# First attention: the head sums, the lead of VectorE's sums and products, and the fetch of rows one by one

## What is computed

```python
h = jnp.maximum(_layernorm(x, axis=-1), 0.0)
x = x + _L0_gnn_ref(h, src, dst, ...)        # gatv2 with 8 heads, layer norm, gatv2 with 1 head, layer norm
h = jnp.maximum(_layernorm(x, axis=-1), 0.0)
x = x + _L1_gnn_ref(h, edge_index, edge_type_34, ...)

def gatv2(x, src, dst, Ws, bs, Wd, bd, attn):
    H, D = attn.shape
    fs = (x @ Ws + bs).reshape(-1, H, D)
    fd = (x @ Wd + bd).reshape(-1, H, D)
    e = jax.nn.leaky_relu(fs[src] + fd[dst], 0.2)
    logits = jnp.einsum('ehd,hd->eh', e, attn)
    m = jax.ops.segment_max(logits, dst, num_segments=N)
    ex = jnp.exp(logits - m[dst])
    denom = jax.ops.segment_sum(ex, dst, num_segments=N)
    alpha = ex / denom[dst]
    out = jax.ops.segment_sum(alpha[:, :, None] * fs[src], dst, num_segments=N)
    return jax.nn.elu(out)
```

## Time and profile before

| | |
|---|---|
| median of 3 runs | 3938.12 us (3933.74 to 3942.07) |
| the profiled execution | 3949.69 us, of it 3948.0 us span |
| busy of the span | TensorE 3111.3 (79%), VectorE 2549.2 (65%), ScalarE 1629.4 (41%), GpSimd 1508.1 (38%) |
| stages, us from the start | first attention 400 to 1090, projections 1090 to 1300, second attention 1300 to 1810, relations 1810 to 3230, last gather 3230 to 3705, the rest to 3948 |

### The profile page before, as it was taken

One profiled execution on the slowest core, in us unless ns is written; L12 is line 12 of the kernel. 1 busy time (PEld: TensorE's weight loads), 2 busy tenths in 40 slices (PEclk: granted clock), 3 DMA queues, 4 the chain that ended last, 5 costly groups with the idle time before them and its releaser, 6 DMA issues. The chain is left out here.

```text
span 3948.0 us, 63256 instructions
## 1 busy us (share of the span) xinstructions
PE 3111.3 (79%) x14356; PEld 2365.0 (60%) x14357; DVE 2549.2 (65%) x5088; ACT 1629.4 (41%) x4996; POOL 1508.1 (38%) x1783
## 2 busy tenths in 40 slices
PE   0196788888869799995669999999999974444699
PEld 0053444444445455553359999999999973444455
DVE  8233799999856788886645555555455548999412
ACT  0010566666622222222324444444444438888400
POOL 0373454545346666662111111111111127777200
PEclk6598899999989899997879999999999986666799
DMA  0233433434354455552145656556555545555300
GB/s 25 78 85 105 130 117 113 123 110 119 97 204 156 154 160 152 157 160 97 48 153 184 184 182 185 171 180 186 177 182 180 180 136 169 176 176 176 132 9 31
DMA packets 181911, 546.64 MB, mean 138 GB/s; under 512 B 37415, under 2 KB 82299, under 8 KB 181563
## 3 DMA queue, kind: packets, MB, share of 16 engines
q0 software_dynamic: 77264, 331.42, 28.1%
q1 hardware_dynamic: 53772, 143.14, 11.9%
q10 hardware_dynamic: 50832, 71.59, 5.0%
HBM read 428.42 MB, written 117.91 MB: 138 GB/s over the span
## 5 line engine op out<-in xcount | busy, mean ns | idle before, releaser
L1795 PE MATMUL pO<-wh,gT 128*128 128x384 f32 x4128 | 1096.8, 339 | 3.7 <-DVE wl L1833 3.7
L1795 PEld LDWEIGHTS pO<-wh,gT 128*128 128x128 f32 x4128 | 752.7, 189 | 4.5 <-DVE wl L1833 4.5
L1795 PE MATMUL pO<-wl,gT 128*128 128x384 f32 x2064 | 692.9, 336 | 0.0
L798 POOL DMA_INDIRECT row<-fs_d,rec x400 | 460.5, 1151 | 385.9 <-PE pA L977 232.1
L1819 DVE TENSOR_SCALAR cntge<-pT 128x768 int32<-128x768 int32 x173 | 165.7, 958 | 574.7 <-PE pT L504 573.8
L511 PE MATMUL pO<-wt,hT 128*128 128x384 f32 (+1 forms) x1200 | 418.9, 511 | 43.0 <-ACT hT L1501 19.6
L1747 ACT ACTIVATE gT<-cntge 128x256 fp32r<-128x256 f32 x1038 | 371.7, 410 | 172.3 <-PE pO L1795 122.8
L923 ACT ACTIVATE sj<-sj 128x96 f32<-128x96 f32 x1176 | 313.2, 268 | 210.3 <-DVE sj L1032 207.4
L1795 PEld LDWEIGHTS pO<-wl,gT 128*128 128x128 f32 x2064 | 390.2, 189 | 0.0
L1757 ACT ACTIVATE nrow<-pO 128x384 f32<-128x384 f32 x344 | 165.9, 482 | 543.1 <-PE pO L1795 543.1
L1927 PE MATMUL pC<-identb,own 128*128 128x128 bf16 x960 | 193.1, 304 | 236.0 <-ACT cntge L1908 121.9
(11 more groups left out here) (335 smaller groups left out, 5686.3 us busy)
## 6 DMA issues: line engine op xcount, KB each, us to landing
raw<-in_L_gnn_W_rel_dram SPq DMA_DIRECT2D x204, 384.0 KB
y_d<-nrow ACTq DMA_DIRECT2D x344, 192.0 KB
y_d<-nothing SPq DMA_DIRECT2D x53, 384.0 KB
row<-fs_d,rec POOLq DMA_INDIRECT x400
kept_d<-fdt ACTq DMA_DIRECT2D x1, 3840.0 KB, 16.3
kept<-kept_d SPq DMA_DIRECT2D x1, 3840.0 KB
fs_d<-of SPq DMA_DIRECT2D x9, 388.0 KB
fd_d<-of SPq DMA_DIRECT2D x9, 388.0 KB, 2.6
```

What stands on the lines that cost most here:

```text
L798: pool.indirect_dma_start(b["row"][u][:, j, :], None, table, bass.IndirectOffsetOnAxis(ap=b["rec"][u][:, 2 * j + field:2 * j + field + 1], ...
L1795: last = pe.matmul(pO[:, q, 0:HALF], gT[:, c, half, :].bitcast(F32R), w[:, c, lo:up].bitcast(F32R), start=c == 0 and k == 0, stop=c == KC ...
```

## The change

Three things in the first attention, and one in the shared gather:

1. ScalarE makes the head sums of all four rows (32 activations a group). VectorE's L1029 goes, and with it the signal `own_ok`. The products come in the order of rows 2, 3, 0, 1, where it was 1, 2, 3, 0.
2. `sj` becomes two buffers. VectorE's `add` and ScalarE's `sums` run for group u+2 in iteration u, not u+1, and once more ahead of the loop. The wait on `logits` is for the group two back.
3. TensorE's program keeps its order: pS of u+2, pA of u.
4. Where `used` counts once a row (first attention and last gather), GpSimd waits for each row's own count before its fetch, not for all four before the first. The second attention keeps its one wait.

The parts that `attention` had for one head go; no call used them.

```diff
-            def rows(u):
+            def rows(u, free=None):
                 for j in range(S):
+                    if free is not None and used.rate == S:
+                        used.wait(pool, *free, j + 1)
+                        pool.sem_inc(b["posted"], 1)
                     pool.indirect_dma_start(b["row"][u][:, j, :], None, table, bass.IndirectOffsetOnAxis(
...
-                    used.wait(pool, i, w - U)
+                    if used.rate == 1:
+                        used.wait(pool, i, w - U)
                     pool.sem_inc(b["posted"], 1)
-                    rows(w % U)
+                    rows(w % U, (i, w - U))
...
-            BY_DVE = 1 if heads > 1 else 0
-
-            ORDER = [*range(BY_DVE, S), *range(BY_DVE)]
+
+            ORDER = [*range(S // 2, S), *range(S // 2)]
...
-                sj = sb("sj", [P, S, D], F32, st)
+                sj = [sb(f"sj{u}", [P, S, D], F32, st) for u in range(2)]
...
                         sums(0, 0)
+                        sums(0, 1)
...
-                                sums(i, u + 1)
+                                sums(i, u + 2)
...
-                                (leaky if heads > 1 else logits).wait(pe, i, off - 1, ORDER.index(S // 2 + j) + 1)
+                                leaky.wait(pe, i, off - 1, ORDER.index(S // 2 + j) + 1)
...
+                            into = sj[off % 2]
                             for j in range(S // 2):
-
-                                if j < BY_DVE:
-                                    leaky.wait(dve, i, off - 1, S)
-                                else:
-                                    logits.wait(dve, i, off - 1, j + 1 - BY_DVE)
-                                dve.tensor_tensor(sj[:, j, 0:D], row[off % U][:, j, 0:D], fd[:, 0:D],
+                                logits.wait(dve, i, off - 2, ORDER.index(j) + 1)
+                                dve.tensor_tensor(into[:, j, 0:D], row[off % U][:, j, 0:D], fd[:, 0:D],
...
-                                if j < BY_DVE:
-                                    dve.scalar_tensor_tensor(scalar=0.0, op0=ALU.max, op1=ALU.mult, **ins)\
-                                       .then_inc(own_ok.sem, 1)
-                                    own_ok.wait(dve, i, off)
-                                    dve.tensor_reduce(dots[off % U][:, j, :], sj[:, j, :].rearrange("p (h d) -> p h d", h=heads),
-                                                      X, ALU.add).then_inc(leaky.sem, 1)
...
+                                dve.scalar_tensor_tensor(scalar=0.0, op0=ALU.max, op1=ALU.mult, **ins)\
+                                   .then_inc(leaky.sem, 1)
...
                         add(0, 0, 0)
+                        second, = sum_tiles(dve, 1, 1, 0)
+                        add(0, 1, second)
...
-                                add(i, u + 1, t[u + 2])
+                                add(i, u + 2, t[u + 3])
```

More of the change, by code:

```diff
@@ L858, in attention @@
                 neg = sb("neg", [P, S], F32, st)
-                sj = sb("sj", [P, S, D], F32, st)
+                sj = [sb(f"sj{u}", [P, S, D], F32, st) for u in range(2)]
                 lin = [sb(f"lin{u}", [P, S, heads], F32, st) for u in range(U)]
                 scaled = sb("scaled", [P, D], F32, st)
-                shares = sb("shares", [P, S, P], F32, st) if heads == 1 else None
                 attr = sb("attr", [P, D], F32, st)
@@ L877, in attention @@
                 leaky = Signal(st, "leaky", S, U, U)
-                own_ok = Signal(st, "own_ok", 1, U, U)
-                logits = Signal(st, "logits", S - BY_DVE, U, U)
+                logits = Signal(st, "logits", S, U, U)
                 ex_in = Signal(st, "ex_in", 1, U, U)
@@ L911, in _ @@
                     def _(act):
-                        for s in (ex_ok, scaled_ok) + ((logits,) if heads > 1 else ()):
+                        for s in (ex_ok, scaled_ok, logits):
                             s.open(act)
                         def sums(i, off):
-                            for j in range(BY_DVE, S if heads > 1 else 0):
-                                leaky.wait(act, i, off, ORDER.index(j) + 1)
-                                if j == BY_DVE:
+                            for k, j in enumerate(ORDER):
+                                leaky.wait(act, i, off, k + 1)
+                                if k == 0:
                                     ex_ok.wait(act, i, off - U)
                                 for h in range(heads):
-                                    of_head = sj[:, j, h * HD:(h + 1) * HD]
+                                    of_head = sj[off % 2][:, j, h * HD:(h + 1) * HD]
                                     last = act.activation(of_head, of_head, ACT.Copy,
@@ L975, in _ @@
                                     for q, lo, up in HB:
-                                        share = ident[:] if heads > 1 else shares[:, j, :]
-                                        last = pe.matmul(pA[:, q, 0:HALF], share, row[u][:, j, lo:up],
+                                        last = pe.matmul(pA[:, q, 0:HALF], ident[:], row[u][:, j, lo:up],
                                                          start=j == 0, stop=j == S - 1)
@@ L982, in _ @@
                     def _(dve):
-                        for s in (sum_ok, leaky, own_ok, ex_in, weighted, top_ok, den_ok, lin_ok) + ((logits,) if heads == 1 else ()):
+                        for s in (sum_ok, leaky, ex_in, weighted, top_ok, den_ok, lin_ok):
                             s.open(dve)
@@ L1019, in add @@
                                     sum_ok.wait(dve, i, off, j + 1)
-                                    ins = dict(out=sj[:, j, :], in0=sj[:, j, :], in1=attr[:])
+                                    ins = dict(out=into[:, j, :], in0=into[:, j, :], in1=attr[:])
                                 else:
                                     sum_pe.wait(dve, i, off, j - S // 2 + 1)
-                                    logits.wait(dve, i, off - 1, j + 1 - BY_DVE)
-                                    ins = dict(out=split(sj[:, j, :]), in0=halves(pS[j - S // 2]), in1=split(attr[:]))
-                                if j < BY_DVE:
-                                    dve.scalar_tensor_tensor(scalar=0.0, op0=ALU.max, op1=ALU.mult, **ins)\
-                                       .then_inc(own_ok.sem, 1)
-                                    own_ok.wait(dve, i, off)
-                                    dve.tensor_reduce(dots[off % U][:, j, :], sj[:, j, :].rearrange("p (h d) -> p h d", h=heads),
-                                                      X, ALU.add).then_inc(leaky.sem, 1)
[L1031 to L1036, removed]
+                                    logits.wait(dve, i, off - 2, ORDER.index(j) + 1)
+                                    ins = dict(out=split(into[:, j, :]), in0=halves(pS[j - S // 2]), in1=split(attr[:]))
+                                dve.scalar_tensor_tensor(scalar=0.0, op0=ALU.max, op1=ALU.mult, **ins)\
+                                   .then_inc(leaky.sem, 1)
                         def finish(i, off, tile):
@@ L1048, in arguments @@
                             logits.wait(dve, i, u)
-                            if BY_DVE:
-                                leaky.wait(dve, i, u, S)
                             lin_ok.wait(dve, i, u)
@@ L1070, in weigh @@
                             for j in range(S):
[L1071 to L1077, removed]
+                                of_heads = row[u][:, j, 0:D].rearrange("p (h d) -> p h d", h=heads)
+                                dve.tensor_tensor(of_heads, of_heads, over(pe_[u][:, 1 + j, :], 2, [P, heads, HD]), ALU.mult)\
                                    .then_inc(weighted.sem, 1)
@@ L1086, in _ @@
                         add(0, 0, 0)
+                        second, = sum_tiles(dve, 1, 1, 0)
+                        add(0, 1, second)
                         turns = dve.value_load(ctl[0:1, C_TURNS:C_TURNS + 1], min_val=1, max_val=MAX_TURNS)
                         with dve.Fori(0, turns) as i:
-                            t = sum_tiles(dve, -1, U + 2, i)
+                            t = sum_tiles(dve, -1, U + 3, i)
                             v = Steps(dve, dve_step, i * (PER * U) + FIRST)
```

## The result

| | before | after |
|---|---|---|
| median | 3938.52 us (3933.74 to 3942.07, 4 runs) | 4098.06 us (4094.85 to 4101.93, 4 runs) |
| span of the profiled execution | 3948.0 us | 4096.5 us |

What follows compares the result with a forecast made beforehand. VectorE was taken to bound the kernel before, at 13.48 us a group. A ring of 15.1 plus 2.1 for the clock gives 17.2; 47 periods less 650.7 add 157.7, the prologue 3: 4099 us, range 3990 to 4130.

Steps and rivals of the forecast that it cites:

- The mechanism: First attention: VectorE and TensorE wait on each other in one ring, with TensorE's clock low after each rest; chance 0.70.
- The loop: First attention's loop: 47 periods of 17.2 us, 808.4 less 650.7, so 157.7 us longer.
- the prologue: Ahead of the first attention's loop: VectorE makes group 1 there too, between none and 6 us, taken as 3.
- The order of the two engines: First attention: TensorE's pS of u+2 comes after pA of u-1, which waits for VectorE's first weighing of u-1.
- The length of the ring: First weighing, pA, pS, four VectorE steps to the next weighing: 15.1 us a turn at TensorE's high clock.
- The clock: TensorE, idle 4.5 us a turn, restarts at the low clock: 2.1 us lost a period, ends 1.6 and 3.0.
- VectorE's own work: First attention: without the head sum, 0.98 us less a group, from 13.48 to 12.5 us.
- ScalarE: First attention: a fourth row of head sums, 8.5 us instead of 6.4, about 11.2 in all, costs nothing.
- Turns of the loop: TensorE's loads of tile numbers between pA and pS cost nothing; other end 1.47 us a turn, 17 in all.
- Gathers row by row: GpSimd's fetch in first attention and last gather: nothing gained or lost; 12 us if each added wait cost 0.06.
- VectorE stays the bound: First attention's loop: pS is ready when VectorE asks, period 12.87, 46 us less, 3895 us in all; chance 0.06.

Runs made afterwards that it cites:

- e7: Changed kernel with half of the weighted sum pA left out (8 matmul instructions of 16): 3999.05 us, 1.0138 of before.
- e8: Kernel before with half of the weighted sum pA left out in the same way: 3938.59 us, 0.9995 of before.
- e2: Changed kernel with VectorE weighing before its sums and products, and ScalarE summing group u+1 instead of u+2: 3903.50 us, 0.9899 of before.
- e1: Changed kernel with six unread filler matmuls (12 instructions) in TensorE's rest between pS and pA: 4015.27 us, 1.0179 of before.
- e3: Changed kernel with the head sum of row 0 back on VectorE and three rows on ScalarE: 4164.65 us, 1.0560 of before.
- e9: Changed kernel with the weighing first, and GpSimd waiting for all four rows before fetching as before: 3878.48 us, 0.9835 of before.
- e6: Kernel before with only the fetch of rows one by one added, in both gathers: 3940.09 us, 1.0002 of before.
- e5: Changed kernel with GpSimd again waiting for all four rows before the first fetch, in both gathers: 4097.88 us, 1.0396 of before.
- e12: Changed kernel with the weighing first and the fetch row by row, same code as e2, run again: 3904.04 us, 0.9899 of before.
- e10: Changed kernel with the weighing first and the fetch row by row, same code as e2, beside e9 on one chip: 3888.15 us, 0.9858 of before.

## Why the prediction was right

Measured 4098.06, predicted 4099, in a range of 3990 to 4130. The mechanism was right; that the number is right within 1 us is partly luck. The loop was predicted 158 us longer and is 152, the prologue 3 and is 3 to 4, which makes some 4094 on the median, and single executions lie 4 us around theirs. Point by point:

- **The order of the two engines** was the step that decided it, and it holds: waits for pS ahead of both products, a wait for the weighing ahead of pA, none between pA and pS. In the rows above VectorE waits 4.5 us a group for pS (2.88 + 1.62), where 4.7 was written down for the low clock. e7 and e8 show it on the path by the same cut, e2 by opening it.
- **The length of the ring**: 15.1 predicted, 15.25 at the high clock in e1. The steps of the engines were right; what was short is the time between them: 0.14 us from the end of the first weighing to pA (717.37 + 0.95 to 718.46), where 0.05 was taken, and 0.12 from the end of pS to the product (712.96 + 0.81 to 713.89), where 0.03 was.
- **The clock**: 2.1 predicted from the eleven rests of that length, 1.8 by e1's comparison. The two misses have opposite signs and partly cancel: 17.2 predicted, 17.08 measured. The share was within 1.6 to 3.0 in each kernel: 1.8 here, 2.2 after e3's longer rest (7.44 - 5.24) and 2.0 in e7. The Trainium skill (TensorE: Matmul & The Clock Gate, "What's actually happening") reckons the ramp as under 1% of a typical span. That does not hold for this kernel: e1 took 83 us away, 2.0% of the span, since the rest recurs in each of 48 groups.
- **VectorE's own work**: 0.98 less a group predicted; e2 and e9 run at 12.45 and 12.49 us from weighing to weighing within a turn, 1.0 under 13.48 to 13.55.
- **ScalarE** would cost nothing in the changed kernel: so it was, e3 being slower with less on ScalarE.
- **Turns of the loop**: taken at nothing; the first group of a turn is no longer than others by more than the clock's variation (16.9 to 17.4 from weighing to weighing all along, but for the very first with 17.6).
- **Prologue**: 3 us more predicted, 2.7 to 4.2 measured. From VectorE's first row sum to its first weighing it is 24.7 us in the changed kernel and 20.5 in e6 and 22.0 in e8, which have before's prologue. The profiled execution of before, with 26.8, seems to say that it became shorter; that is its wait of 7.22 us, which e6 and e8 do not have.
- **Gathers row by row**: 0 in both stages, by e5 and e6.
- Working out the rival "VectorE stays the bound" as 3895 gave the number that the opened ring then nearly had with the fetch row by row: 3888 to 3904 (3878 with the whole fetch).

## What to carry to other kernels

When one engine's work is moved a step ahead, write down for each of its inputs between which two pieces of the producer's program that input is made; if the producer does something first that waits for the consumer's own last step, the lead has closed a ring, and its length, not any engine's load, is the period. The cure can lie on the consumer's side alone: doing the step that releases the producer first (here the weighing) and the leading work last gave the lead back without touching TensorE. A rest of 4.7 us in each period is also paid for by TensorE's clock, here with 1.8 us of 17. And before a small difference between two profiles is read, a sibling kernel's profile of the same stretch is worth a look: one late start of 6 us had the prologue's sign reversed here.

## What the runs showed of the hardware that was not expected

- Idle matmuls paid: 12 extra instructions a group, 4.03 us of TensorE's time, took 1.8 us off the period by keeping the clock at 1.00 (e1).
- The fetch row by row cost nothing in two kernels (e5, e6) and 10 and 26 us in a third (e9 to e12), where ScalarE starts later at the loop's turn. In the four kernels without traffic ahead of the turn that start took 0.6 to 0.9 us, in the three with traffic there 1.9 to 3.6.
- The same kernel gained 1.42% on one chip and 1.01% on two others (e10, e2, e12), nearly all in the first group of each turn: 13.4 to 13.9 us against 14.4 to 15.9. Why the chips differ is open. With the whole fetch the two chips agreed within 1 us.
